# A gated delta-rule layer with routed experts: the last chunk's inverse levels moved ahead, and the output work shared out differently

## The reference, cut to what matters

```python
xn = layernorm(x)                                  # x: [2, 2048, 256]
q, k, v = heads(xn @ Wq), heads(xn @ Wk), heads(xn @ Wv)   # H=4, DK=128, DV=64
beta = sigmoid(xn @ Wb); k = k * rsqrt(sum(k*k) + 1e-12); q = q * DK**-0.5
def step(S, inp):                                  # over all 2048 positions
    delta = (v_t - einsum('bhk,bhkv->bhv', k_t, S)) * b_t[..., None]
    S = S + k_t[..., :, None] * delta[..., None, :]
    return S, einsum('bhk,bhkv->bhv', q_t, S)
o = o * rsqrt(mean(o*o) + 1e-5) * norm_w * silu(xn @ Wg)
s = o.reshape(b, n, H*DV) @ Wo
e = argmax(softmax(xn @ router_w.T))               # one of 8 experts per token
y = square(relu(xn @ fc[e])) @ proj[e]             # hidden width 1024
out = x + s * silu(y)
```

## Time and profile before

| | |
|---|---|
| median of 3 runs | 806.24 us (805.21 to 806.88) |
| the profiled execution | 805.54 us |
| its span, first to last instruction | 803.8 us |
| mean granted TensorE clock | 0.977 |
| TensorE busy | 764.4 us, 95% of the span |
| VectorE, GpSimd, ScalarE busy | 531.9, 393.3, 345.8 us |
| DMA | 116.25 MB, mean 145 GB/s |

### The profile page before, as it was taken

The page is one execution under the profiler, slowest core; times in us unless marked ns, Lnnn a source line. Parts: engine busy times, 40 slices in busy tenths (PEclk is TensorE's granted clock), DMA queues, the critical chain, the costliest instruction groups (busy, mean ns, idle before and its releaser), DMA issues.

```text
span 803.8 us, 22106 instructions
## 1 busy us (share of the span) xinstructions
PE 764.4 (95%) x8970; PEld 649.3 (81%) x8970; DVE 531.9 (66%) x1159; ACT 345.8 (43%) x754; POOL 393.3 (49%) x407
## 2 busy tenths in 40 slices
PE   6969999999999999999999999999999999999953
PEld 5957888888888888888888888888787878788842
DVE  6786565655756556575565777676777676777577
ACT  4823434444443445344444444444443435354420
POOL 3725472535526354363544646364636474655411
PEclk9999999999999999999999999999999999999955
DMA  9608634425343253333623423232333333230087
GB/s 301 212 1 340 236 113 194 150 112 177 135 163 128 113 222 132 121 126 120 234 115 118 148 91 126 112 125 108 126 112 126 113 118 120 95 144 8 21 284 247
DMA packets 37748, 116.25 MB, mean 145 GB/s; under 512 B 3664, under 2 KB 24400, under 8 KB 27664
## 3 DMA queue, kind: packets, MB, share of 16 engines
q1 hardware_dynamic: 33904, 104.62, 35.3%
q0 software_dynamic: 3744, 10.23, 3.9%
HBM read 101.33 MB, written 13.50 MB: 143 GB/s over the span
## 4 chain that ended last, share of the span: by engine, by line
PE 88%; DVE 5%; POOL 3%; issue 2%; DMA 1%; another core or an unknown queue 1%; ACT 1%; DVEq 0%; POOLq 0%; SPq 0%
PE bank L466 18%; PE bank L477 16%; PE bank L542 7%; PE bank L510 7%; PE bank L495 6%; PE bank L442 4%; PE bank L440 4%; PE bank L441 4%; PE bank L681 4%; PE bank L577 3%; PE bank L587 3%; PE bank L597 2%; POOL ImM L2055 2%; PE bank L397 2%; PE bank L522 2%
## 5 line engine op out<-in xcount | busy, mean ns | idle before, releaser
L477 PE MATMUL bank<-wts,hT 128*128 128x256 f32 x624 | 172.2, 393 | 0.0
L466 PE MATMUL bank<-xsT,wts 128*128 128x128 f32 x1248 | 167.1, 281 | 0.1
L466 PEld LDWEIGHTS bank<-xsT,wts 128*128 128x128 f32 x1248 | 150.8, 192 | 10.9 <-issue 10.7
L1507 DVE TENSOR_TENSOR Pm<-bank,lvl_mask 128x256 f16<-128x256 f32 x192 | 72.5, 419 | 70.1 <-PE bank L577 69.2
L2036 POOL TENSOR_TENSOR XTl<-f_t,XTh 128x512 f16<-128x512 f32 x32 | 41.1, 1292 | 153.9 <-DVE XTh L1450 153.8
L1043 ACT CAST Z<-bank 128x256 f16<-128x256 f32 x192 | 63.2, 376 | 121.3 <-PE bank L597 121.3
L1518 DVE TENSOR_TENSOR M<-bank,M 128x256 f16<-128x256 f32 x192 | 73.3, 418 | 58.2 <-PE bank L587 57.5
L477 PEld LDWEIGHTS bank<-wts,hT 128*128 128x128 f32 x624 | 104.9, 191 | 7.0
L987 ACT ACTIVATE hT<-bank 128x512 f32<-128x512 f32 x78 | 46.7, 598 | 47.9 <-PE bank L466 47.6
L510 PE MATMUL bank<-xT,wq_sb 128*128 128x128 f32 x512 | 63.0, 276 | 0.0
L542 PE MATMUL bank<-wvg_sb,xT 128*128 128x512 f32 x128 | 62.9, 614 | 0.0
(11 more groups left out here) (213 smaller groups left out, 1930.5 us busy)
## 6 DMA issues: line engine op xcount, KB each, us to landing
wts<-in_fc SPq DMA_DIRECT2D x39, 1024.0 KB
wts<-in_pj SPq DMA_DIRECT2D x39, 1024.0 KB
wts<-in_x SPq DMA_DIRECT2D x10, 512.0 KB, 9.3
wts<-y_d SPq DMA_DIRECT2D x4, 1024.0 KB, 9.3
out_x<-wts SPq DMA_DIRECT2D x16, 256.0 KB, 2.2
xn_d<-wts SPq DMA_DIRECT2D x3, 1024.0 KB, 4.4
x_first<-in_x SPq DMA_DIRECT2D x4, 512.0 KB, 17.3
wts<-in_x SPq DMA_DIRECT2D x4, 256.0 KB, 3.5
```

The costliest lines, as they stand in the source:

```text
L466: ins = pe.matmul(psum[bank[n]][:, (c % 4) * P:(c % 4 + 1) * P], fcw[r][:, k, c * P:(c + 1) * P], xsT[:, k, :], start=(k == 0), stop=(k == ...
L477: ins = pe.matmul(psum[bank[0]][:, 0:D], hT[:, c, :], pjw[r][:, c, :], start=(c == 0), stop=(c == HC - 1))
L1507: dve.tensor_tensor(h4(Pm, b).rearrange("p h (n c) -> p h n c", c=s), half4(b).rearrange("p h (n c) -> p h n c", c=s), mask, ALU.mult).the ...
```

## The change

Three groups of edits. First, the levels of the last chunk (15) get buffers, PSUM banks and semaphores of their own: `M` and `Z` in the space of `wk_sb`, `Pm` in that of `wq_sb`, the banks `KG_BANK`, and semaphores used before for the first loads. So they no longer wait for the levels of chunk 14 to be done; `MZ(15)` waits for `K` and `Q` of chunk 15, and `M0(15)` for `P32` of chunk 15. `ImM_` has one more wait. Second, the step list changes: eight steps of three tiles, four of two; steps 13 and 14 and the tail, with five tiles (34 to 38), are written out in one order per engine. Third, x's second half is loaded after tile 36 into ring slot 0, ahead of the y loads (y now takes slots 1 and 2), and `add_x` of chunks 0, 2, 4, 6, 8, 9, 10 and 12 runs on GpSimd, with one semaphore for each engine's adds (the last function of the diff is GpSimd's). The four loads of x's second half are taken out behind the y loads.

```diff
-        FIRST_TILES, STEPS = 2, [3] * 7 + [2] * 7
-        assert FIRST_TILES + sum(STEPS) + 2 == NT
+        FIRST_TILES, STEPS = 2, [3] * 8 + [2] * 4
+        assert FIRST_TILES + sum(STEPS) + 5 == NT
...
+        last16 = wk_sb[:].rearrange("p k n -> p (k n)").bitcast(F16).rearrange("p (z h n) -> p z h n", z=2, h=NS)
+        Ms, Zs = [M, last16[:, 0]], [Z, last16[:, 1]]
+        Pms = [Pm, wq_sb[:, 0, 0:NS * P // 4].bitcast(F16).rearrange("p (h n) -> p h n", h=NS)]
...
-        yf = wts[:, 0:4 * W].rearrange("p (c n) -> p c n", c=NCH)
+        yf = wts[:, 2 * W:6 * W].rearrange("p (c n) -> p c n", c=NCH)
-        x_last = wts[:, 4 * W:6 * W].rearrange("p (c n) -> p c n", c=NCH // 2)
+        x_last = wts[:, 0:2 * W].rearrange("p (c n) -> p c n", c=NCH // 2)
...
-        ON_POOL = []
+        ON_POOL = [0, 2, 4, 6, 8, 9, 10, 12]
...
+        def level_bank(m, b):
+            return KG_BANK[b] if last(m) else b
+
+        def stage_of(eng, m, l, b, sems, last_sems):
+            if last(m):
+                eng.wait_ge(last_sems[b], LAST_FROM[b] + l + 1)
+            else:
+                At(eng, m).stage(NL, l, sems[b])
...
+                sp.wait_ge(wt_in[0], 32 * (NT // RING))
+                At(sp, NT - RING).on(yp)
+                xl = x_last.rearrange("p c (b d) -> p b c d", b=B)
+                for k in range(GROUPS // 2, GROUPS):
+                    n = CG * (k - GROUPS // 2)
+                    for b in range(B):
+                        sp.dma_start(xl[:, b, n:n + CG], x_v[b, :, CG * k:CG * (k + 1), :]).then_inc(xf_in[1], 16)
...
                 for c in range(NCH):
-                    sp.wait_ge(out_ok, c + 1)
+                    sp.wait_ge(out_pool if c in ON_POOL else out_dve, added(c))
...
                 def M0(m):
                         lv.on(Z0_ok[b])
-                        lv.on(dZf_ok[b], back=1)
+                        if last(m):
+                            lv.on(P32_ok[b])
+                        else:
+                            lv.on(dZf_ok[b], back=1)
...
                 def MZ(m, b):
+                    if last(m):
+                        lv.on(*Kp, *Qp)
+                    else:
+                        lv.on(Up, F_ok[b], back=1)
...
                 def ImM_(m, b):
+                    stage_of(pool, m, NL - 1, b, dM_ok, last_dM_ok)
+                    lv.on(F_ok[b], back=1)
...
                 def add_x(c):
+                    pool.wait_ge(ys_ok, c + 1)
+                    pool.wait_ge(xf_in[c // (NCH // 2)], 16 * B * GROUPS // 2)
+                    pool.tensor_tensor(chunk_of(c), chunk_of(c), x_of(c), ALU.add).then_inc(out_pool, 1)
```

More of the change, by code:

```diff
@@ L259, in build_program, with added @@
         rows_ps = psum[LG_BANK][:, 0:2 * NT].rearrange("p (z j) -> p z j", z=2)
-        ON_POOL = []
+        ON_POOL = [0, 2, 4, 6, 8, 9, 10, 12]
+        def added(c):
+            return sum(1 for n in range(c + 1) if (n in ON_POOL) == (c in ON_POOL))
         def steps(step3, step2):
@@ new lines, in tail @@
+                    Zc(13)
+                    experts(3)
+                    U(13)
+                    K(15, 0)
+                    experts(2)
+                    M0(14)
+                    Q(15, 0)
+                    L(14, 0)
+                    O(13)
+                    Dm(14, 0)
+                    experts(4)
+                    T(14, 0)
+                    dS(13)
+                    experts(2)
+                    L(14, 1)
+                    experts(1)
+                    Q(15, 1)
@@ new lines, in tail @@
+                    keep_y(34)
+                    q_h(14, 1)
+                    dZ(13, 2, 0)
+                    dZ(13, 2, 1)
+                    y_sigmoid(34)
+                    ogTc(12)
+                    relu(35, 1)
+                    relu(35, 0)
+                    kTc(14, 0)
+                    dZ(13, 3, 0)
+                    dZ(13, 3, 1)
+                    kTc(14, 1)
+                    sq(35, 0)
+                    sq(35, 1)
+                    s_cp(12)
+                    sig(14, 0)
@@ L1512, in dM @@
                     s = LEVELS[l]
[L1513 removed]
+                    stage_of(dve, m, l, b, dMp, last_dMp)
                     if l == 0:
@@ L1827, in tail @@
                 def tail():
+                    R32(12)
+                    R_h(12)
+                    R_l(12)
+                    MZ(13, 0)
+                    MZ(13, 1)
+                    Zo(13, 0)
+                    Zo(13, 1)
+                    U_h(12)
+                    U_l(12)
+                    Pm_(13, 0, 0)
+                    Pm_(13, 0, 1)
+                    dM(13, 0, 0)
+                    kss_(14, 1)
+                    dM(13, 0, 1)
+                    og_(12)
+                    kss_(14, 0)
@@ new lines, in tail @@
+                    Pm_(13, 5, 1)
+                    X_h(14, 0)
+                    R32(13)
+                    dM(13, 5, 0)
+                    dM(13, 5, 1)
+                    P32(14, 1)
+                    R_h(13)
+                    P32(14, 0)
+                    Fr_(13, 0)
+                    P_h(14, 1)
+                    Fr_(13, 1)
+                    v(14, 1)
+                    gate_(14, 1)
+                    R_l(13)
+                    P_h(14, 0)
+                    MZ(14, 0)
@@ new lines, in tail @@
+                    MZ(14, 1)
+                    Zo(14, 0)
+                    Zo(14, 1)
+                    U_h(13)
+                    kss_(15, 0)
+                    U_l(13)
+                    kss_(15, 1)
+                    Pm_(14, 0, 0)
+                    Pm_(14, 0, 1)
+                    dM(14, 0, 0)
+                    dM(14, 0, 1)
+                    og_(13)
+                    f_t(15, 0)
+                    q_l(15, 0)
+                    oss_(13)
+                    k_h(15, 0)
@@ L2164, in tail @@
                 def tail():
+                    krn_(14)
+                    orn_(12)
+                    k_l(14, 0)
+                    rows(36)
+                    ogm(12)
+                    rows(37)
+                    k_l(14, 1)
+                    X_l(14, 1)
+                    gate_y(34)
+                    X_l(14, 0)
+                    ImM_(13, 0)
+                    ImM_(13, 1)
+                    send_y(34)
+                    P_l(14, 0)
+                    P_l(14, 1)
+                    root_(14)
+                    krn_(15)
+                    k_l(15, 0)
+                    orn_(13)
+                    k_l(15, 1)
+                    ogm(13)
+                    rows(38)
+                    X_l(15, 0)
+                    gate_y(35)
+                    send_y(35)
+                    X_l(15, 1)
+                    gate_y(36)
+                    send_y(36)
+                    P_l(15, 0)
                     gate_y(37)
-                    orn_(14)
-                    ogm(14)
+                    ImM_(14, 1)
+                    ImM_(14, 0)
+                    P_l(15, 1)
                     send_y(37)
```

503 lines of the change are left out of this document (354 added, 149 removed).

## The result

| | before | after |
|---|---|---|
| median | 805.73 us (4 runs, 805.02 to 806.88) | 799.21 us (4 runs, 798.41 to 799.55) |
| profiled execution, its span | 805.54, 803.8 us | 798.41, 796.7 us |
| mean granted TensorE clock | 0.977 | 0.986 |

What follows compares the result with a forecast made beforehand. TensorE's work bounds until the last expert matmul, then chunk 15's chain and VectorE's output queue together. Span 758.7 + 25.1 + 13.4 + 1.2 + 2.6 = 801.0, plus 2.4 gives 803.4 us; range 799.0 to 808.0.

Steps and rivals of the forecast that it cites:

- T: End of the last matmuls on the last expert tile in the kernel before, at 761.37 us.
- Part 1, T': New end of the last expert matmul: 761.4 - 4.5 + 0.9 = 757.8 us, 758.7 with one TensorE stall.
- a third tile in step 8 costs and brings nothing: TensorE's dense stretch before the last expert matmul: the same matmuls in another order, so no gain or cost.
- the stall that I took: One TensorE wait of 0.88 us where two chunks' levels mix, raising 757.8 to 758.7 us.
- Part 2: Chunk 15's chain from the last expert matmul to og(15): 25.1 us, against 28.1 before.
- a full clock "ends at 801": TensorE's clock staying full in the tail: end at 801, counted inside the forecast without a chance of its own.
- Part 3: Eight adds moved to GpSimd take turns with VectorE: 13.4 us after og(15) against 10.0, late by 3.8 us.
- Part 4: x's second half loaded ahead of the y loads: outputs start earlier, worth nothing at the end.
- (a): GpSimd's adds do not hold VectorE, so chunk 15's chain sets the end: 799.8 us, chance 0.17.
- (b): Clock falls earlier; at half level VG and wo(14) cost 1.9 and 0.9 us more: 806.2 us, chance 0.22.
- (c): Two chunks' levels do not interleave before the last expert matmul: eight stalls, 7.0 us, 809.5 us, chance 0.15.
- (d): Chunk 15's levels do not come ahead, as its masks wait for its front part; folded into (c).

Runs made afterwards that it cites:

- The last experiment: Changed kernel with VG(15,1) ahead of the last three expert units instead of behind them: 800.8 us, 0.9936 of before.
- that of R32: Changed kernel with R32, R_h and R_l of chunk 15 ahead of weigh(2) instead of behind it: 799.03 us, 0.9909 of before.
- the fourth experiment: Kernel before with only the eight adds moved to GpSimd, nothing else changed: 808.8 us, 1.0043 of before.
- The step-list experiment: Kernel before with only the step list changed (third tile in step 8, one tile left for the tail): 807.29 us, 1.0018 of before.
- first experiment: Changed kernel with all 16 adds back on VectorE: 802.69 us, 0.9965 of before.
- The four-add experiment: Changed kernel with only adds 0, 2, 4, 6 on GpSimd, 8, 9, 10, 12 back on VectorE: 797.04 us, 0.9896 of before.

## Why the prediction was right or wrong, point by point

**What bounds it.** Right: TensorE's work up to T, then VectorE's queue and chunk 15's chain. The last experiment and that of R32 show which of the two is left after the change. An R32(15) that starts 0.9 us earlier brings 0.3 us in the profile and nothing that the times can tell, and a first weigh that starts 1.8 us later costs 1.6: the end follows VectorE's stream, which starts with the first y load.

**Part 1, T'.** The step "a third tile in step 8 costs and brings nothing" failed, together with the stall that I took. TensorE was dense as predicted. Its waits from 97 to 761 us, after (engine, line, waited for: us, times, longest):

```profile
PE bank L645 <- ACT Z L1180: 1.1, 4, 0.3
PE bank L600 <- DVE Z L1714: 0.9, 2, 0.8
PE bank L633 <- DVE wk_sb L1733: 0.4, 1, 0.4
PE bank L600 <- issue: 0.3, 1, 0.3
PE bank L615 <- ACT wk_sb L1180: 0.2, 1, 0.2
```

and before:

```profile
PE bank L609 <- ACT Z L1043: 2.0, 7, 0.3
PE bank L563 <- DVE Z L1498: 1.3, 2, 0.8
```

The two waits on wk_sb (where the change puts chunk 15's M and Z) stand behind the last expert matmul, in level 4:

```profile
758.47 0.62 PE L633 MATMUL bank<-ident,wk_sb 128*128 128x64 f16 x8 [0.40 <-DVE wk_sb L1733]
759.32 0.61 PE L615 MATMUL bank<-wk_sb,XTh 128*128 128x64 f16 x8 [0.22 <-ACT wk_sb L1180]
```

So up to T' TensorE never waited for a level of chunk 15: the overlap cost no stall there, where I had taken one of 0.9. Without the stall the sum was 757.8, so 1.6 us are left to explain. The starts of KS on TensorE give them. A two-tile step lasts 42.52 us (612.12 to 654.64 before), and a three-tile step 49.12 (441.84 to 490.96 after): the third tile costs 6.6 us. Its own matmuls, by the chain's rows of 533 to 543 us in the kernel before, are more:

```profile
536.49 1.42 PE bank L466 x12
...
540.21 1.81 PE bank L477 x8
...
542.78 0.22 PE bank L449 x2
```

32 of the first, 16 of the second and two transposes are 3.8 + 3.6 + 0.2 = 7.6 us. So a two-tile step carries 1.0 us in which TensorE is not fed. Of it the trace shows 0.3 as idle, the wait for Z that stands seven times in the list above; the stretch of one such step of before:

```profile
484.55:527.07 42.52, 42.19 (x523) 35.33 (x521) 30.60 (x65) 18.65 (x42) 23.05 (x22) 1.00 0.30 113
```

A matmul's latency counts as busy, and so covers short gaps. That 0.7 us are hidden in the busy count is worked out, not seen. The starts of KS(11) show what step 8 won: from KS(0) it is 515.2 us before (612.12 - 96.91) and 521.8 after (619.02 - 97.25), so the tile took 6.6 of its 7.6 us there and 1.0 was saved. From KS(11) to the last expert matmul it is 149.3 us before and 137.2 after, 12.0 less. The tile that left (7.6) and the 3.6 of the sum are 11.2 of it, so 0.8 more was saved in steps 13, 14 and the tail, where two two-tile steps with their 1.0 us each had stood. Less 0.3, by which chunk 0's KS starts later after, that is 1.5 of the 1.6. What became of the other 1.2 us of those two steps I did not separate.

T' itself is as uncertain as that start. In the ten kernels whose TensorE order is the same up to it, it lies between 755.99 and 757.71, but always 659.0 to 659.1 us behind chunk 0's KS. Before, that distance is 664.5, and 663.9 in the kernel of the fourth experiment, with the same front.

The step-list experiment has the same 6.6 us (442.89 to 492.0, then steps of 42.5), yet its tail lost its density. So the saving at the front did not reach the end without the overlapped levels.

**Part 2, the tail's chain.** Predicted T'+25.1, measured T'+23.15. The terms that failed are those ahead of R32(15), where I took a clock between its two levels: dZ(15,5) ended at T'+7.6 (8.8 taken, from a level that ran at the half clock), F took 0.9 (1.8), wo(14) 1.95 (2.9), KS 0.9 (1.3). KS ended at T'+11.95, not T'+15.4. TensorE in this stretch, beside the earlier trace rows:

```profile
764.62 1.95 PE L717 MATMUL bank<-wo_sb,ogT 128*128 128x256 f32 x8
...
767.33 0.19 PE L473 MATMUL bank<-S_h,kT 128*128 128x64 f16 x1 [0.32 <-ACT xT L1201]
```

The clock stayed at 1.00 until 771 us. TensorE was busy for 4.97 of the 5.76 us behind the last expert matmul (756.24 to 762) and for 5.56 of the next 6, with VG(15,1), the transpose, F and wo(14) there; before, it was busy for 3.91 of 5.63 us (761.37 to 767) when the clock fell. That this denser work is what kept the clock up is argued, not shown: no run takes F or wo(14) away, and with VG(15,1) moved out the clock stayed up as well, to 772 us. The prediction had this case (a full clock "ends at 801") but sized the sum between the two levels.

The R chain then took 3.4 us rather than 2.1, and gave 1.3 of these 3.5 us back: 1.0 by the new wait, 0.3 by a held cast. R32(15) began at 769.18, behind three weighs, while KS had ended at 768.2. The prediction names this case ("if the clock stayed full throughout it would bind, by under 2 us"). By its last sentence a forecast with R32 waiting on a y load would be wrong in kind. The wait is there, but in the R32 experiment it is worth 0.2 us in the medians and 0.3 in the profiles, inside the intervals; that sentence gave it too much weight. The cast R_h took 0.99 us beside a GpSimd add and 0.43 without (first experiment, 768.98). From R_l's end (771.60) to og's (779.39) it took 7.8 us, where 1.5 + 1.3 + 2.8 + 0.6 + 1.4 = 7.6 were taken.

**Part 3, the adds.** Right, in mechanism and size: 13.4 us predicted behind og(15), 13.1 measured. Five VectorE ops were held there, one by ogm(15) and four by the adds, and the last weigh started 4.2 us after s_cp(15) where about 4 was written. The four-add experiment gives 0.55 us an add for those behind ogm. What the prediction did not have is the first four: I called them nearly free. In after, three of the four hold something (three weighs in 2.97 us, R_h in 0.99, a weigh in 1.75), and only the one at 772.89 runs beside PSUM readers. Gated behind U and O, two adds were free. What the four cost in all is small: 797.04 us with them (the second experiment), 796.28 and 795.82 with all adds on VectorE and ogm(15) let in or moved, kernels of different chips.

The Trainium skill (SBUF — State Buffer, Who interferes with whom) says that a VectorE op with at most one SBUF input doesn't contend with GpSimd, outside the two-port modes, and that one with two SBUF inputs does. The rows agree on both: 0.68 and 0.69 beside a 1.26 us add for R_h and R_l from PSUM, 1.75 for the weighs. The cast of R_h from `ru`, float32 in SBUF to float16 in SBUF, has one SBUF input too and was held (0.99 against 0.43); whether it ran in such a mode no run here shows. The Trainium skill (SBUF — State Buffer, SBUF: two separate sides) also says that whoever starts first holds the shared ports for the whole instruction while the other waits. Read so, a wait would end with one instruction. The 10.25 us of ogm(15) in the first experiment span 15 VectorE instructions, which that rule does not explain.

**Part 4, x's second half.** Right, worth nothing, shown by undoing it: 799.11 against 799.21.

**The rivals.** (a), adds that hold nobody, is refuted by the 1.75 us rows and by the 3.7 us that they cost the kernel before. The time came within 0.6 us of (a)'s 799.8 by other means. (b), a clock that falls early, is refuted by wo(14)'s 1.95 us. (c), levels that don't interleave, is refuted: no wait for a level of chunk 15 ahead of the last expert matmul. (d) falls with it.

## What to carry to other kernels

When work is moved from the end of a pipeline to an earlier step, price what it costs there by the difference of two step lengths in the trace, not by its instructions: a step that looks 99% busy still took a third tile for 1.0 us less than its matmuls. Before an engine is relieved by another that takes turns with it, look at what stands behind the moved op in the end stretch; put such ops where the first engine's ops read PSUM, and move the one short op that the chain needs (here the multiply of og) off the contested engine instead. If the end is set by two things at once, judge each part by undoing it alone where that can be done: here the adds were worth about +2.9 us and x's second half 0, which leaves about -9.5 for the levels and the step list, and the whole showed only the sum.

## What the runs showed of the hardware that was not expected

**An op of GpSimd can be kept out by an unbroken VectorE stream.** In three kernels in which VectorE ran weighs and adds (two SBUF inputs, one every 0.60 us), ogm(15) took 10.25, 10.85 and 9.64 us, until a pause of some 0.1 us or the end of the adds; where VectorE was made to wait for it, it took 1.83. In the kernel before, after and those near it, it got in at the first boundary, in 1.10 to 1.21 us. Neither the order of weighs and adds, nor a GpSimd op shortly before, nor the offset of its start from the next VectorE op tells the two apart: that offset was 0.24 us in the first experiment (778.94, then 779.18) and 0.23 in after (780.88, then 781.11). What decides it stays open: much the same stream kept ogm out with no add on GpSimd or with add 6, and let it in with adds 0, 2, 4 and 6 there, and in the kernel before with none. Until it is known, an op of the critical chain on GpSimd beside such a stream is a risk of 9 us, which a wait or a place on VectorE takes away.

**The granted clock** stayed at 1.00 for 15 us behind the last expert matmul, with TensorE 7.75 of 10 us busy from 760 to 770. TensorE was busy for 0.19 us from 768 to 771 us, and then the clock fell:

```profile
768.00:770.00 2.00, 0.19 (x7) 0.07 (x3) 1.97 (x3) 0.17 (x1) 1.37 (x2) 1.00 1.10 358
770.00:771.00 1.00, 0.00 (x0) 0.00 (x0) 0.97 (x2) 0.00 (x0) 0.60 (x1) 1.00 1.09 346
```

With VG(15,1) taken out of this stretch (the last experiment) wo(14) still took 1.95 us, full speed, and the clock stayed at 1.00 until 772 us, 13 us behind the last expert matmul.
